# Two fused LoRA layers on one core: the last form stores go ahead of the ring loads, the token loads of chunk 1 go behind the stacks

## What is computed

```python
# layer 0; layer 1 has the same form with its own weights
c    = x @ Wc.T + bc + scale[id] * ((x @ A[id].T) @ B[id].T)      # adapter by batch entry
base = c @ W.T + b
w    = top2_softmax(c @ Wr.T)                                     # (token, expert)
h    = einsum('td,erd->ter', c, lora_A)
x    = x + base + 2 * einsum('ter,eor,te->to', h, lora_B, w)
```

## Time and profile before

| | |
|---|---|
| median of 3 runs | 712.48 us (709.4 to 714.24) |
| the profiled execution | 710.91 us, span 709.2 us |
| busy: PE | 694.1 us, 98% of the span |
| busy: DVE, ACT, POOL | 408.8 us, 218.8 us, 258.1 us |
| granted TensorE clock, mean | 0.99 |
| DMA | 148.13 MB, mean 209 GB/s |

### The profile page before, as it was taken

How to read it: one execution, slowest core, us unless ns; L and a number is a source line. 1 busy time by engine, 2 the same in 40 slices (tenths; PEclk the granted TensorE clock), 3 DMA queues, 4 the chain that set the end, 5 groups by cost and what they waited for, 6 DMA issues and landing times.

```text
span 709.2 us, 9245 instructions
## 1 busy us (share of the span) xinstructions
PE 694.1 (98%) x3360; PEld 608.2 (86%) x3360; DVE 408.8 (58%) x664; ACT 218.8 (31%) x391; POOL 258.1 (36%) x214
## 2 busy tenths in 40 slices
PE   6999999989999999999999999999899999999997
PEld 6999999877888787888899999998678887878886
DVE  5554576497645376652573654674867436746413
ACT  6334334252212033220504244343432302422200
POOL 0362113070783050493134322120637534207820
PEclk9999999999999999999999999999999999999999
DMA  8254767994678936257832853799837786444633
GB/s 325 71 163 167 261 197 233 336 347 158 199 246 284 315 105 209 86 154 239 315 117 72 267 162 135 241 349 293 305 113 237 270 315 207 149 148 140 196 110 119
DMA packets 74595, 148.13 MB, mean 209 GB/s; under 512 B 7604, under 2 KB 38452, under 8 KB 74550
## 3 DMA queue, kind: packets, MB, share of 16 engines
q1 hardware_dynamic: 70998, 139.01, 58.6%
q10 hardware_dynamic: 2016, 6.42, 2.7%
q0 software_dynamic: 1536, 2.10, 1.0%
HBM read 98.42 MB, written 47.32 MB: 205 GB/s over the span
## 4 chain that ended last, share of the span: by engine, by line
PE 92%; DMA 4%; SPq 2%; DVE 1%; issue 1%; ACT 0%
PE ps L459 28%; PE ps L460 28%; PE ps L461 28%; PE ps L534 3%; DMA form_scratch<-f_hl 3%; PE ps L583 2%; DMA a_hl<-form_scratch 1%; SPq L346 1%; PE ps L555 1%; PE ps L476 1%; DMA w_raw<-in_w 1%; DVE bw_st L898 0%; PE ps L565 0%; SPq L348 0%; PE ps L551 0%
## 5 line engine op out<-in xcount | busy, mean ns | idle before, releaser
L459 PE MATMUL ps<-x_hl,a_hl 128*128 128x512 f32 x448 | 177.1, 395 | 5.5 <-DMA a_hl<-form_scratch 5.5
L460 PE MATMUL ps<-x_hl,a_hl 128*128 128x512 f32 x448 | 175.8, 392 | 0.0
L461 PE MATMUL ps<-x_hl,a_hl 128*128 128x512 f32 x448 | 175.7, 392 | 0.0
L459 PE MATMUL ps<-e_hl,w_hl 128*128 128x388 f32 (+1 forms) x432 | 149.0, 345 | 6.0 <-DVE e_hl L898 6.0
L460 PE MATMUL ps<-e_hl,w_hl 128*128 128x388 f32 (+1 forms) x432 | 148.5, 344 | 0.0
L461 PE MATMUL ps<-e_hl,w_hl 128*128 128x388 f32 (+1 forms) x432 | 148.2, 343 | 0.0
L459 PEld LDWEIGHTS ps<-x_hl,a_hl 128*128 128x128 f32 x448 | 84.9, 190 | 23.4 <-issue 5.9
L461 PEld LDWEIGHTS ps<-x_hl,a_hl 128*128 128x128 f32 x448 | 84.9, 190 | 18.1
L460 PEld LDWEIGHTS ps<-x_hl,a_hl 128*128 128x128 f32 x448 | 84.8, 189 | 17.5
L459 PEld LDWEIGHTS ps<-e_hl,w_hl 128*128 128x128 f32 x432 | 82.8, 192 | 6.0 <-DVE w_hl L898 6.0
L460 PEld LDWEIGHTS ps<-e_hl,w_hl 128*128 128x128 f32 x432 | 83.1, 192 | 0.0
(11 more groups left out here) (111 smaller groups left out, 944.8 us busy)
## 6 DMA issues: line engine op xcount, KB each, us to landing
a_hl<-form_scratch SPq DMA_DIRECT2D x112, 512.0 KB, 4.2
form_scratch<-f_hl SPq DMA_DIRECT2D x56, 512.0 KB, 7.1
e_raw<-in_ext SPq DMA_DIRECT2D x12, 580.0 KB, 8.2
w_raw<-in_w ACTq DMA_DIRECT2D x12, 512.0 KB, 3.4
x_raw<-in_xT SPq DMA_DIRECT2D x6, 1024.0 KB, 7.2
x_raw<-x_scratch SPq DMA_DIRECT2D x6, 1024.0 KB, 7.6
x_scratch<-x_raw SPq DMA_DIRECT2D x16, 256.0 KB, 3.3
out_T<-x_raw SPq DMA_DIRECT2D x16, 256.0 KB, 2.8
```

The costliest lines, as they stand in the source:

```text
L459: nc.tensor.matmul(dst, w_hi, m_hi, start=start, stop=False, skip_group_check=again)
L460: nc.tensor.matmul(dst, w_hi, m_lo, start=False, stop=False, skip_group_check=again)
L461: return nc.tensor.matmul(dst, w_lo, m_hi, start=False, stop=stop, skip_group_check=again)
```

## The change

In the stretch of SP's program at the end of the fold, in both layers, the order of issue is rewritten. The last three form stores (places 4 to 6) move from behind the `bw` stores to the place behind ring load 1. The load of B12 moves from there to the place behind stack 0, and ring load 4 goes in front of it. Ring load 5 now follows the `bw` stores, then comes the load of B22, which stood in front of stack 1, then ring load 6. No wait, transfer or instruction is added or taken away; `load_ring` keeps its own waits.

```diff
                 for n in range(2):
                     load_ring(l, 0, n)
-                load_x(l, 0, B12)
+                store_forms(l, KH - 1, range(4, NM))
                 for n in range(2, 4):
                     load_ring(l, 0, n)
                 sp.wait_ge(S["bwr_done"], l + 1)
                 sp.wait_ge(S["bw_lo"], NOB * (l + 1))
                 first_stack(l, 0)
-                load_x(l, 0, B22)
+                load_ring(l, 0, 4)
+                load_x(l, 0, B12)
                 first_stack(l, 1)
                 sp.dma_start(bw_dram[l], bw_st[2 * LOW:P, :, 0:D + ER].bitcast(f32)).then_inc(S["d_bw"], 16)
                 sp.dma_start(bwr_dram[l], bwr[2 * LOW:P, :]).then_inc(S["d_bw"], 16)
-                store_forms(l, KH - 1, range(4, NM))
-                for n in range(4, NM):
-                    load_ring(l, 0, n)
+                load_ring(l, 0, 5)
+                load_x(l, 0, B22)
+                load_ring(l, 0, 6)
```

## The result

The changed kernel takes 707.11 us (median of 11 runs, 703.73 to 710.01), the kernel before 711.67 beside it (11 runs, 709.4 to 714.24). The ratio is 0.994, with a 95% interval of 0.9922 to 0.9959: 4.3 us less, and within 1%. The profiled execution took 707.65 us, its span is 706.0. Of all executions behind the numbers of this document one, of `e12_b12_early`, took 988.97 us at a granted clock of 0.66; its ratio leaves it out.

What follows compares the result with a forecast made beforehand. TensorE, busy 98%, was taken as the bound, with 9.0 us of slot 4 waits and low clock to win. A gain of 4.75 less 1.75 for low clock gave 3.0: 712.48 - 3.0 = 709.5 us, range 704.5 to 713.5.

Steps and rivals of the forecast that it cites:

- (a): At ring slot 4, ahead of W2: early stores remove TensorE's waits of 2.14 and 3.34 us and their low clock.
- 9.0 us: Most the change can win: slot 4 waits of 2.14 + 3.34 plus low clock of 2 x 1.75, or 1.3%.
- (b): SyncE's queue: B22 lands at 151.9 and 500.9, with two more ring loads ahead than today's 19.2 us set.
- An order of issue is an order of landing: SyncE's full queue: transfers land as issued, so moving one forward moves another back by its length.
- (c): Ahead of W2: bwr_scratch lands at 148.0 and 497.0, so 0.1 and 1.3 us of TensorE idling stay.
- TensorE would be there at 148.55: Start of W2, layer 0: the time TensorE would reach it without the slot wait, 150.70 - 2.14.
- (d): At L583, low_and_experts: lb_lo stands 8.6 to 9.7 us after B22's landing; 0.9 to 2.0 us of stall come back.
- (e): At L583, and elsewhere in layer 1: remaining idling brings low clock in one of two layers, costing 1.75 us.
- (f): Behind L583, to chunk 1's adapters (L551): VectorE's distance shrinks from 15.0 to 8.9 us, only just covered, put at nothing.
- all of it comes: Rival at L583: lb_lo is not waited for; 6 to 9 us gained, 703.5 to 706.5; chance 0.16.
- the wait changes its name: Rival at L583: B22 1 us late, both layers fall to low clock; gain about 0, 711 to 713.5; chance 0.19.
- The slower rival: Rival at L583: B22's later landing delays it in each layer; at 3 us, 4.7 us slower, 717; chance 0.07.

Runs made afterwards that it cites:

- e12_b12_early: The changed kernel with B12's load put back ahead of ring load 2, so ahead of stack 0; 715.21 us, ratio 1.0048 to the kernel before.
- e2: The changed kernel with the lb_hl cast (ACT) and subtraction (VectorE) ahead of B22's in super-chunk 0; 706.76 us, ratio 0.9936.
- e4: The changed kernel with GpSimd made to wait for lb_lo ahead of make_t3; 710.93 us, ratio 1.002.
- e3: The changed kernel with two of the three stores (W3, W7) moved from ahead of ring load 2 to behind ring load 4; 707.16 us, ratio 0.9957.
- e1: The kernel before with only the three stores moved, to behind ring load 1; 714.58 us, ratio 1.0064.
- e8: The changed kernel unchanged, measured and profiled a second time; 707.28 us, ratio 0.9954 to the kernel before.
- e11: The same kernel as e6 (B22's load alone moved), run again on another chip; 702.42 us, ratio 0.988.
- e6: The kernel before with B22's load alone moved, behind the last stores and ring load 4; 703.31 us, ratio 0.9895.
- e7: The changed kernel with store W7, B12 and B22 issued later, and lb and chunk 1's adapters earlier on ACT and VectorE; 710.07 us, ratio 0.9991.
- e5: e2 with the adapters of chunk 1 also ahead of T3's split on ACT and VectorE; 707.39 us, ratio 0.9961.
- e9: e6 with ring load 5 also ahead of B22, lb_hl's split ahead of B22's, chunk 1's adapters ahead of T3's; 705.87 us, ratio 0.9928.
- e10: e7 with T2's split ahead of the adapters of chunk 1 again on ACT and VectorE; 704.48 us, ratio 0.9905.

## Why the prediction was right, and where it was not

A gain of 3.0 us was forecast, 4.3 came (2.9 to 5.6 by the interval), and the difference is within 1% as said. The time itself, 707.11, lies in the range of 704.5 to 713.5 and 2.4 below the point; 0.8 of that is the kernel before, whose median came out at 711.67 and not 712.48. The mechanism, a removed stall part of which returns at `low_and_experts` because B22 is late, is shown by e2 and e4. Step by step:

**(a) The slot waits go.** Right. TensorE waits for no slot, and SP's new wait for a store costs 0.9 us in all, off the path. The worth put on it, "9.0 us", was slightly too large: low clock costs 1.4 a stretch, not 1.75. I had taken L583's start from the chain, 163.45, where the timeline has 163.29, and 11.0 for W2 at full clock, where 11.2 is measured. 8.3 is the right ceiling.

**(b) B22 at 151.9 and 500.9.** It landed at 152.62 and 499.46:

```profile
x_raw<-in_xT SPq DMA_DIRECT2D x1, 1024.0 KB, 13.9
```

(issued 138.76 in layer 0, by the list of transfers). Counting the set of transfers ahead of it works. From the landing of ring load 1, where the forecast counted from, it said 21.8 us; the change's two profiles have 22.6 and 22.9, and 22.6 and 21.9. Measured from the short matmuls the spread is wider, within about 2 us: the forecast is 33.8 and 35.1, the profiles have 35.7 and 34.7, and 34.6 and 33.6. "An order of issue is an order of landing" is not true of the small parts, though: three parts of stack 0, issued from 129.34 on, land at 136.7 to 138.6, ahead of ring load 3, which was issued at 128.74 and lands at 139.2.

**(c) `bwr_scratch` at 148.0 and 497.0, W2 waiting 0.1 and 1.3.** It landed at 148.83 and 495.68; ACT's copy followed at once in layer 0:

```profile
148.90 2.06 ACT L812 COPY u<-ps 128x512 f32<-128x512 f32 x4 [0.70 <-DMA bwr_scratch<-bwr]
```

Layer 1 waits 1.30 us, as said. In layer 0 W2 starts at 149.99 without a wait of its own, but only because TensorE had already lost 2.49 us and a low stretch at L552. "TensorE would be there at 148.55" is the part that failed. In the second profile it is the other way round: 1.21 us of wait in layer 0 and none in layer 1.

**(d) `lb_lo` 8.6 to 9.7 behind B22.** Right, and it is the step on which the forecast stood: L584 starts 9.44 and 9.45 behind it in the change, 9.4 in both layers of its second profile. The set beside GpSimd takes 6.38 (6.8 forecast), `lb` 2.31, just above the upper bound of 2.2. The returned waits are 0.90 and 1.33, then 1.34 and 1.35 (0.9 to 2.0 forecast). e12 shows the limit: VectorE must be free when B22 lands.

**(e) One low stretch of two.** Right in number in the first profile only, and wrong in place and in what it costs. It lies behind L552's 2.49 us, not at L584; the 0.90 to 1.35 us there were never followed by low clock, and the second profile has no low stretch behind a wait at all. The 1.75 us taken off for it were not lost in either profile, since L584 starts 9.4 us behind B22 with the stretch and without it.

**(f) The rest is covered.** Barely. At the change's order no wait appears at the adapters of chunk 1; once L584 comes 1.0 and 2.0 us earlier (e2), they are 0.57 and 0.56 late.

**The step that was missing.** I followed slot 4, `bwr_scratch` and B22 through the queue, and not stack 0, which moved too: the change puts 1.5 MB of stores in front of it and takes 1 MB of B12 away, 1.3 us by my own lengths. Measured from the short matmuls, its last part landed at 21.2 and 22.6 us before, at 24.3 and 23.0 after. TensorE had 2.1 us of slack there in layer 0 before, partly thanks to a low stretch in the fold, and 0.7 in layer 1. That shows as 3.65 us of waits and one low stretch in the first profile, 1.1 us in the second. It did not set the end in the change, where B22's landing does: in e3 stack 0 is in time and nothing is gained. e1 and e12, with 1 MB more ahead of stack 0, show what it costs once it does set the end.

**Where the number was lucky.** The sum was 4.75 - 1.75 = 3.0; the ruler's stretches gain 2.4 us in the first pair and 4.6 with the second profile, 3.5 on average. By L584 = landing of B22 + 9.44 this comes out as 4.75, less 0.4 for B22 (on average 1.3 us late in layer 0 and 0.9 early in layer 1, from the short matmuls), less 0.6 because `lb_lo` falls at 9.44 and not at the middle of 8.6 to 9.7, less 0.3 because L583 started 0.16 us earlier per layer before than the chain says. The 1.75 of (e) is in none of it: a wrong loss stood in for three small ones. And the 0.4 is small only because ring load 1, ahead of the change, landed 1.0 us earlier than before in the mean of the two sums; counted from there B22 is 1.4 us late over both layers.

Nor did the gain come in the form that was said. By the working, idling was to go from 5.5 us to about 4.3 and one of the two low stretches behind the slot waits was to stay; measured, idling is 7.2 and 5.0, and three of four low stretches are gone, two of them in the fold in the first profile and one in the second. I do not count those in the fold as a source: layer 1 of e8 has one and is 1.16 us shorter than layer 1 of after without it, and in layer 1 the last store lands 27.4 us behind the short matmuls in e11, which has one, and 27.5 in e6, which has none. Where a transfer sets the end, a slower TensorE ahead of it only waits less. That this holds for the kernel before as well is argued, not shown: no profile of it lacks these stretches.

Of the rivals, "all of it comes" fell (e2 and e4 show the `lb` wait), "the wait changes its name" was right on the waits alone: 7.2 and 5.0 us for 5.5, while the low clock went from four stretches to one. The slower rival did not come; a late transfer does make this kernel slower in e1 and e12, but it is stack 0, not B22.

## What to carry over

On a full queue each transfer moved forward pushes back all that it passes, so list every transfer passed with the time at which TensorE asks for it, the small ones too; one that is left out can decide, as stack 0 does in e1 and e12. Rather than bringing the late transfer forward, look for one that is far too early and take it out of the way: B22, moved alone, gave 1.2% where the whole reordering gave 0.6%. And in these runs several idle pieces of about 1 us were cheaper than one of 2 to 4, which had low clock behind it. Last, count from the landing of the last transfer that did not move: two profiles of one kernel differ by over 1 us before the change begins.

## What the runs showed of the hardware

- Idling and low clock. Waits of TensorE of 1.69 us and less in these stretches were not followed by low clock; 1.86 (e4), 1.97 (e2), 2.04 (e3), 2.14, 2.22 (e7), 2.35 (e4) and 2.49 were, and 3.23, 3.37 and 4.03 (e1, e12) by two stretches in a row. It is not a clean order: 1.86 in e4 also had two stretches behind it, and the 2.41 of e1 and the 3.34 of before only one. A stretch costs 1.4 us.
- The 18 short bias matmuls (2.06 us, TensorE counted as busy) are the same in all kernels, and are followed by low clock in some executions and not in others: in both layers of before, in none of after, in layer 0 alone in e5, e9 and e10, in layer 1 alone in e8 and e11.
- Two-input subtractions of VectorE beside GpSimd take 1.6 to 1.7 us each instead of 0.62; the one over 1024 elements 2.31 instead of 1.23.
- On the full queue the order of landing was the order of issue for ring loads, form stores and token blocks, but not for the small transfers. Parts of 144 KB overtook a ring load of 512 KB issued ahead of them (landed at 136.7 to 138.6 and at 139.2 in the changed kernel), while the smallest were the last: 1 KB of `rlog`, issued behind those parts, took 9.6 us and landed at 141.2; 2 KB of `bwr` took 12.0. Why is open.
